# Two masked attention layers on one core: fewer, larger on-chip transfers, paired weighted sums, and a moved projection block

## The reference, cut to what matters

```
q = latents @ q_w + q_b ;  kv = [x, latents] @ kv_w + kv_b        # layer 0
attn = softmax(q k^T / 32, masked) ; o = attn @ v ; o @ out_w + out_b + residual
rmsnorm -> gelu MLP -> + residual
a = layer_norm(ctx) ; Q = h Wq^T ; K, V = a Wk^T, a Wv^T          # layer 1
softmax(Q K^T / sqrt(32), masked) @ V, then Wo^T, times tanh(gate), + h
```

## Time and profile before

| | |
|---|---|
| runs, median (lowest to highest) | 2631.36 us (2630.4 to 2631.77), 3 runs |
| profiled execution | 2632.31 us, its span 2630.5 us |
| busy in the span | PE 93%, PEld 73%, ACT 56%, DVE 44%, POOL 9% |
| layer 0, MLP, layer 1 | about 0 to 1070 us, to 1823 us, to the end |

### The profile page before, as it was taken

How to read it: one execution, slowest core, us unless ns; L and a number is a source line. 1 busy time by engine, 2 the same in 40 slices (tenths; PEclk the granted TensorE clock), 3 DMA queues, 4 the chain that set the end, 5 groups by cost and what they waited for, 6 DMA issues and landing times. The chain is left out here.

```text
span 2630.5 us, 43959 instructions
## 1 busy us (share of the span) xinstructions
PE 2443.7 (93%) x14528; PEld 1913.9 (73%) x14528; DVE 1170.5 (44%) x2222; ACT 1472.5 (56%) x3354; POOL 226.2 (9%) x252
## 2 busy tenths in 40 slices
PE   6999999999999999899999999998888888888887
PEld 5677777777777777478888888887767677676674
DVE  4455555555555555452212221122655455455553
ACT  3777777777777777552222222222556566566564
POOL 1000000000000000000000000001211112112110
PEclk8999999999999999799999999999999999999998
DMA  6555555555555555341101110121566665656655
GB/s 173 106 114 113 113 113 113 113 113 113 109 115 112 112 112 97 76 140 49 48 0 48 48 48 0 48 80 64 106 130 124 118 138 102 127 131 109 132 100 86
DMA packets 172764, 255.82 MB, mean 97 GB/s; under 512 B 33793, under 2 KB 84257, under 8 KB 172721
## 3 DMA queue, kind: packets, MB, share of 16 engines
q1 hardware_dynamic: 172720, 255.27, 45.3%
HBM read 86.28 MB, written 25.21 MB: 42 GB/s over the span
## 5 line engine op out<-in xcount | busy, mean ns | idle before, releaser
L531 ACT ACTIVATE l_score_ps<-l_score_ps,l_neg_max 128x512 f32<-128x512 f32 (+1 forms) x1024 | 566.6, 556 | 338.3 <-DVE l_neg_max L696 337.9
L696 DVE TENSOR_REDUCE l_neg_max<-l_score_ps 128x1 f32<-128x512 f32 (+1 forms) x768 | 494.6, 684 | 149.7 <-PE l_score_ps L934 149.3
L544 ACT ACTIVATE l_probs<-l_score_ps 128x1024 f32<-128x1024 f32 x384 | 385.0, 1020 | 104.5 <-PE l_score_ps L959 103.0
L934 PE MATMUL l_score_ps<-l_stack 97*128 97x512 f32 (+1 forms) x1024 | 326.9, 379 | 80.4 <-DMA l_stack<-mask_rows 53.2
L1220 ACT ACTIVATE mlp_hidden<-mlp_hidden_ps,mlp_b_col 128x512 f32<-128x512 f32 x128 | 88.3, 690 | 496.2 <-PE mlp_hidden_ps L66 496.0
L959 PEld LDWEIGHTS l_score_ps<-l_stack 99*128 99x128 f32 x1536 | 213.9, 194 | 156.5 <-issue 81.6
L1255 DVE TENSOR_TENSOR mlp_hidden_l<-mlp_hidden,mlp_hidden_h 128x512 fp32r<-128x512 f32 x128 | 93.7, 732 | 518.3 <-ACT mlp_hidden_h L1222 518.3
L959 PE MATMUL l_score_ps<-l_stack 99*128 99x256 f32 x1536 | 277.7, 308 | 40.7 <-ACT l_probs L544 25.4
L934 PEld LDWEIGHTS l_score_ps<-l_stack 97*128 97x128 f32 x1024 | 181.4, 202 | 126.3 <-ACT l_score_ps L531 63.3
L974 PE MATMUL l_o_ps<-l_probs,l_v 128*32 128x256 f32 x3072 | 244.5, 398 | 1.8
L713 DVE TENSOR_TENSOR l_o_norm<-l_o_ps,norm_room 128x256 f32<-128x256 f32 x128 | 54.4, 425 | 401.0 <-PE l_o_ps L974 318.1
(11 more groups left out here) (128 smaller groups left out, 4195.8 us busy)
## 6 DMA issues: line engine op xcount, KB each, us to landing
l_stack<-room SPq DMA_DIRECT2D x256, 192.0 KB
l_stack<-l_qk SPq DMA_DIRECT2D x256, 128.0 KB
l_stack<-room SPq DMA_DIRECT2D x128, 128.0 KB
norm_room<-l_shiftT SPq DMA_DIRECT2D x512, 32.0 KB, 4.0
l_stack<-l_qk SPq DMA_DIRECT2D x256, 64.0 KB
l_tokens<-in_x SPq DMA_DIRECT2D x16, 512.0 KB, 4.1
l_tokens<-in_ctx SPq DMA_DIRECT2D x16, 512.0 KB, 5.0
l_stack<-room SPq DMA_DIRECT2D x128, 64.0 KB
```

The costliest lines, as they stand in the source:

```text
L531: m = act.activation(e, e, ACT.Exp, bias=neg_max[:, q, h:h + 1], accum_out=row_sum[:, q, h:h + 1])
L544: act.activation(probs[:, s % PROBS, :].rearrange("p (a b) -> p a b", a=2), score_ps[:, 2 * (s % 2):2 * (s % 2) + 2, :], ACT.Exp).then_inc ...
L696: dve.tensor_reduce(out, bank, AXIS_X, ALU.max, negate=True).then_inc(max_done, 1)
L934: m = pe.matmul(out, stack[0:ROWS_MAX, h, P * q:P * (q + 1)], stack[0:ROWS_MAX, h, K_COLS], start=True, stop=True)
```

## The change

`load_stacks` becomes `load_group`: the columns of the query and key weights are stored permuted (`by_dim`), so that the four heads of a group lie on 128 partitions in the order of the stack, and one DMA moves what four DMAs moved for a half of the groups. A batch has 16 (layer 0) or 12 (layer 1) such DMAs in place of 32, and each group is loaded as soon as its own steps are done. The two shift DMAs of a half become one, the eight inverse DMAs two, each of four neighbouring rows spread over 128 partitions. The second pass goes by pairs of steps. In the last slot shifted 0 and 1 and `turn_shift` of half 1 stand ahead of the projection block, and ACT does exps 0, the copy, exps 1 ahead of the block's `high`. The permuted weights split in four DVE instructions instead of one, and layer 0's bias vectors load in 11 DMAs instead of 5.

```diff
-    PROBS = 3
+    PROBS = 4
-    STACK_DMAS = HG * 4 + 1
+    GROUP_DMAS = 4 if first else 3
+    STACK_DMAS = GROUP_DMAS * GROUPS + 1
...
+        def by_dim(w):
+            return w.rearrange("p f (g d j) -> p (f g) j d", d=DH, j=HG)
+        def by_head(w):
+            return w.rearrange("p f (g j d) -> p (f g) j d", d=DH, j=HG)
...
+                return [*[(bq[:, f:f + 1], q_b[f]) for f in range(FB)],
+                        *[(bk[:, f:f + 1], k_b[f, :, :, 0]) for f in range(FB)], (bv[:, :], kvb[:, :, 1]),
...
-        VECTORS = 5 if first else 3
+        VECTORS = 2 * FB + 3 if first else 3
-        INV_DMAS = HALF
+        INV_DMAS = GROUPS
...
-        def load_stacks(sp, b, half):
-            def move(slot, j, to_cols, src):
-                heads = slice(HALF * half + j, HALF * (half + 1), HG)
+        def load_group(sp, g):
+            half, heads = g // GROUPS, slice(HG * g, HG * (g + 1))
+            def move(slot, to_cols, src):
                 sp.dma_start(f32(stack[DH * slot:DH * (slot + 1), heads, to_cols]), f32(src)
                              ).then_inc(stack_loaded[half], 16)
+            if first:
+                move(0, Q_COLS, qk[:, g, Q_HIGH])
+                move(0, K_COLS, qk[:, g, K_HIGH])
+            else:
+                move(0, slice(0, WIDTH), qk[:, g, :].rearrange("p (n s) -> p n s", s=S)[:, 0:4:3, :])
+            move(1, slice(0, WIDTH), qk[:, g, 0:WIDTH])
+            move(2, slice(0, WIDTH), qk[:, g, WIDTH:2 * WIDTH])
...
-            def spread_inverse(a, half):
+            def spread_inverse(p, a, half):
+                if p is not None and half == HALVES - 1:
+                    sp.wait_ge(low_done, ITEMS * (p + 1))
...
-                for j in range(HALF):
-                    g, to = GROUPS * half + j // HG, slice(DH * (j % HG), DH * (j % HG + 1))
-                    sp.dma_start(inv_sum[to, g:g + 1, :],
-                                 shiftT[INV_ROW + j:INV_ROW + j + 1, half:half + 1, :].to_broadcast([1, DH, S])
+                for g in range(GROUPS * half, GROUPS * (half + 1)):
+                    row = INV_ROW + HG * (g % GROUPS)
+                    sp.dma_start(inv_sum[:, g, :], shiftT[row:row + HG, half:half + 1, :].to_broadcast([HG, DH, S])
                                  ).then_inc(inv_loaded[half], 16)
...
-                        for part in range(2):
-                            sp.dma_start(
-                                f32(stack[SHIFT_ROW + part:SHIFT_ROW + part + 1,
-                                          HALF * half:HALF * (half + 1), Q_COLS]),
-                                shiftT[HALF * part:HALF * (part + 1), half:half + 1, :],
-                            ).then_inc(shift_loaded[half], 16)
+                        sp.dma_start(f32(stack[SHIFT_ROW:SHIFT_ROW + 2, HALF * half:HALF * (half + 1), Q_COLS]),
+                                     shiftT[0:2 * HALF, half:half + 1, :]).then_inc(shift_loaded[half], 16)
...
-                            sp.wait_ge(shifted_done, PSTEPS * a + PSTEPS // HALVES * (half + 1))
-                        load_stacks(sp, p, half)
+                            sp.wait_ge(shifted_done, PSTEPS * a + KB * (g + 1))
+                        load_group(sp, g)
+                        if g % GROUPS == GROUPS - 1:
+                            load_mask(sp, p, g // GROUPS)
...
+                    if slot == SLOTS and a is not None:
+                        exps(a, 0)
+                        copy_shift(a, HALVES - 1)
+                        exps(a, 1)
...
+                    if slot == SLOTS - 1 and a is not None:
+                        shifted(a, 0)
+                        shifted(a, 1)
+                        turn_shift(a, HALVES - 1)
...
-                    for s in range(PSTEPS):
-                        if s + 2 < PSTEPS:
-                            shifted(a, s + 2)
+                    for s in range(0, PSTEPS, 2):
+                        for u in range(s + 2, min(s + 4, PSTEPS)):
+                            shifted(a, u)
                         weigh(a, s)
-                        if s >= KB and s % KB == KB - 1 and s < PSTEPS - 1:
-                            project(a, s // KB - 1)
+                        weigh(a, s + 1)
+                        if s >= KB and s % KB == KB - 2 and s < PSTEPS - 2:
+                            g = s // KB - 1
+                            if g == 0:
+                                if p is not None:
+                                    pe.wait_ge(low_done, ITEMS * (p + 1))
...
+                            project(a, g)
```

More of the change, by code:

```diff
@@ L236, in attention_layer @@
                     kv = stage[c].rearrange("p (f n two) -> p f n two", f=2, two=2)
[L237 to L240, removed]
+                    src, parts = kv[:, :, :, which], [t[:, 2 * c:2 * c + 2, :] for t in w]
+                    if w is wk:
+                        src, parts = by_head(src), [by_dim(t) for t in parts]
+                    split_ops.append((c, src, parts, 1.0))
+            staged = [stage[u % 2].rearrange("p (f n) -> p f n", f=FB) for u in range(4)]
+            split_ops.append((3, by_head(staged[3]), [by_dim(t[:, :, :]) for t in wq], SCALE))
+            split_ops.append((2, staged[2], [t[:, :, :] for t in wo], 1.0))
         else:
@@ L247, in attention_layer @@
                     n = FB * u + f
-                    split_ops.append((u, score_ps[:, n % RING, :], [t[:, f, :] for t in w], scale))
+                    src, parts = score_ps[:, n % RING:n % RING + 1, :], [t[:, f:f + 1, :] for t in w]
+                    if u < 2:
+                        src, parts = by_head(src), [by_dim(t) for t in parts]
+                    split_ops.append((u, src, parts, scale))
         last_op_of = [max(n for n, op in enumerate(split_ops) if op[0] == u) for u in range(len(raw))]
@@ L305, in load_tokens, with load_mask @@
             sp.dma_start(tokens[:, QT:2 * QT, :], c_view[b]).then_inc(tokens_loaded, 16)
-        def load_stacks(sp, b, half):
-            def move(slot, j, to_cols, src):
-                heads = slice(HALF * half + j, HALF * (half + 1), HG)
+        def load_group(sp, g):
+            half, heads = g // GROUPS, slice(HG * g, HG * (g + 1))
+            def move(slot, to_cols, src):
                 sp.dma_start(f32(stack[DH * slot:DH * (slot + 1), heads, to_cols]), f32(src)
                              ).then_inc(stack_loaded[half], 16)
[L313 to L318, removed]
+            if first:
[5 more added lines that the diff above has]
+            move(2, slice(0, WIDTH), qk[:, g, WIDTH:2 * WIDTH])
+        def load_mask(sp, b, half):
             sp.dma_start(f32(stack[MASK_ROW:MASK_ROW + 1, HALF * half:HALF * (half + 1), K_COLS]),
@@ L392, in iteration @@
                 if p is not None:
-                    for half in range(HALVES):
+                    for g in range(FB):
                         if a is None:
-                            sp.wait_ge(low_done, ITEMS * p + NT + NK + half + 1 if first
-                                       else ITEMS * p + NT + GROUPS * (half + 1))
-                        else:
-                            sp.wait_ge(shifted_done, PSTEPS * a + PSTEPS // HALVES * (half + 1))
-                        load_stacks(sp, p, half)
+                            sp.wait_ge(low_done, ITEMS * p + (NT + NK + g // 2 + 1 if first else NT + g + 1))
+                        else:
+                            sp.wait_ge(shifted_done, PSTEPS * a + KB * (g + 1))
+                        load_group(sp, g)
+                        if g % GROUPS == GROUPS - 1:
+                            load_mask(sp, p, g // GROUPS)
                 if a is not None and not first:
@@ L535, in copy_shift @@
                 act.wait_ge(shift_turned, HALVES * a + half + 1)
-                at_least(act, shift_loaded[half], 32 * a)
+                at_least(act, shift_loaded[half], 16 * a)
                 at_least(act, inv_loaded[half], 16 * INV_DMAS * a)
@@ L573, in iteration @@
                     if a is not None:
-                        for half in range(HALVES):
-                            if TURN_SLOT[half] == slot - 1:
-                                copy_shift(a, half)
+                        if TURN_SLOT[0] == slot - 1:
+                            copy_shift(a, 0)
                         if first and slot == AFTER_T:
@@ L588, in iteration @@
                 if a is not None:
-                    for s in range(PSTEPS):
+                    for s in range(2, PSTEPS):
                         exps(a, s)
@@ L625, in split_low @@
                 dve.wait_ge(w_high, n + 1)
+                if len(src.shape) == 4:
+                    for j in range(HG):
+                        m = dve.scalar_tensor_tensor(low[:, :, j, :], src[:, :, j, :], scale, f32(high[:, :, j, :]),
+                                                     ALU.mult, ALU.subtract)
+                    m.then_inc(w_low, 1)
+                    return
```

(19 more changed lines are left out.)

9 lines of the change are left out of this document (5 added, 4 removed).

## The result

The changed kernel takes 2827.53 us (2825.88 to 2828.26), the kernel before in the same comparison 2631.57 us: a ratio of 1.074, 95% interval 1.072 to 1.076. The forecast was 2677 (2560 to 2704): the right sign, a quarter of the size, and outside the range. The profiled execution of the changed kernel spans 2826.5 us.

What follows compares the result with a forecast made beforehand. TensorE's queue, busy 93% of the span, was taken to set the time. 2632.3 us profiled + 39 (layer 1) + 2 (layer 0) + 5 (setup) = 2678 profiled, 2677 as a median; range 2560 to 2704.

Steps and rivals of the forecast that it cites:

- Half a stack in layer 1 is 1.5 MB, 7.7 us at 201 GB/s: Layer 1's merged stack DMAs keep the old pace, so half 0 is in at 2250.9 and half 1 follows 7.7 us later.
- Stack half 0 is ready about when step 0 wants it: Layer 0's stack adds no wait at step 0; layer 0 in all +0.15 us a batch, +2 us for 15 batches.
- Pairs: Second pass, steps taken two at a time: 0.25 us less a pair, net -1.15 us a batch in layer 0, -0.75 in layer 1.
- The moved block: Projection block behind shifted 0 and 1: shifted 2 starts +0.6 us (0 to 1.2) in layer 0, 0 in layer 1.
- The merged inverses: Four-row spreads, two DMAs a half: 9.7 us a half at 27 GB/s, one DMA after the other.
- Shifted 4: Layer 1: TensorE waits 3.4 us for half 1's shift rows, queued behind half 0's inverses, in place of 1.01.
- step 0 of layer 1: Half 0 of the stack is in at 2250.9, so step 0 starts there, +3.2 us against 2247.7.
- Layer 1 in all: Layer 1 batch +2.6 us (+0.9 to +3.9), for 15 batches +39 us (14 to 58).
- The setup: Start of program: six more vector DMAs +4 us (0 to 9), weights split in four DVE pieces +1 (0 to 3).
- The first: Rival 1, faster: spreads still overlap, 7.2 us a half, 2583 us; read side by side 2541; chance 0.36.
- The second: Rival 2, slower still: new idle time keeps TensorE at 1.2 GHz for longer, +25 us, 2702 us; chance 0.09.

Runs made afterwards that it cites:

- the two-row set: Transfers alone, nothing of the reference computed: 256 KB of spreads as 4 DMAs of two rows each; measured at a DMA share of 0.12.
- the old set: Transfers alone, nothing of the reference computed: 2.36 MB in the old stack DMAs, 32 neighbouring partitions read and 32 written; 11.5 us.
- the slow sets: Transfers alone: 2.36 MB of 3 KB rows, reading every fourth or every second partition, or merged; 126 to 143 GB/s.

## Why the prediction was wrong

**The step that failed** is the one that gave the merged stack DMAs the old pace: "Half a stack in layer 1 is 1.5 MB, 7.7 us at 201 GB/s", and for layer 0 "Stack half 0 is ready about when step 0 wants it". The 201 GB/s were read off 16 DMAs that take 32 neighbouring partitions to 32; the new ones take 128 to 32. The trace of before did not show such an operation, and its price got no bounds, though the spreads beside it, of unseen shape too, did. Alone a half's 2.36 MB take 18.8 us instead of 11.5, and in the kernel 3 KB packets take 0.389 us against 0.229.

**Why that cost so much.** Counted from the issue of half 0's shift in layer 0, step 0 of the changed kernel wants its half at 34.1 us (590.08 - 6.21 - 549.77), of the kernel before at 33.0. The last landing of that half and the time when it is wanted, on the same count, over the nine to eleven batches of each trace between 290 and 1000 us:

| kernel | half 0 in | wanted | layer 0 batch |
|---|---|---|---|
| before | 28.9 to 29.1 | 33.0 | 66.0 |
| merged stack alone | 31.5 to 34.0 | 33.0 to 33.2 | 66.5 |
| pairs, block, merged inverses, old stack | 29.4 to 32.8 | 32.7 to 33.9 | 66.1 |
| every transfer cut up, new layout | 33.2 to 35.0 | 32.9 to 34.4 | 67.5 |
| the change with one-row spreads | 32.0 to 35.8 | 32.4 to 34.1 | 68.4 |
| the change with 16 stack DMAs | 34.7 to 37.2 | 32.9 to 34.1 | 71.3 |
| all of the change | 37.4 to 40.8, 40.3 in the batch above | 32.9 to 34.1 | 75.1 |

There were 4 to 5 us of slack. The slow stack uses up to 4.9 of them, the late inverses with pairs and block up to 3.7, and either alone is almost free in a layer 0 batch. Together they are 11.2 us, 6.2 past the need. That is 2.6 more than the two added. The packets account for it: the merged stack alone stood behind one-row spreads, at 0.32 us, and in the whole change it takes 0.389, and for 2.36 MB, 768 rows of 3 KB on 16 engines, that makes some 3 us (an estimate). Behind such a wait TensorE runs at 1.2 GHz in place of 2.4 for a while (a mean of 0.74 in this window):

```profile
590.00:597.00 7.00, 6.92 (x23) 5.58 (x24) 4.79 (x9) 4.47 (x13) 0.00 (x0) 0.74 1.05 130
```

In the changed kernel the inverses are in at 571.9, 22 us after the shift. At 201 GB/s a half would take 11.7 us from there (2.36 MB) and be in at 583.6, against a need of 583.9: with the old pace "about when step 0 wants it" would have been true, and in the run with the old stack in layer 0 alone the half is in 29.5 to 32.9 us after the shift. That run puts a size on it: 2827.5 - 2683.8 = 144 us, with 151 between forecast and result. In both layers the old stack takes back 178 us, and the 2649 us that are left are 28 under the forecast: the other terms together were too dear.

**By its other steps.** Pairs: layer 0 -1.2 a batch where -1.15 was forecast; layer 1 +0.1 where it was -0.75. There the stack set the end in any case, so that time won ahead of it became wait: the stack waits rose from 53.2 to 73.8 us. The moved block: +1.7 in layer 0 (66.5 against 64.8) where +0.6 stood, and +0.35 in layer 1 for 0; the mechanism, the wait for half 0's shift rows, was right, the wait 2.05 instead of 1.6, and the block gave nothing in return. The merged inverses: a set takes 9.6 us where 9.7 was taken, at 27 GB/s and a DMA share of 0.20. The Trainium skill, "DMA: Bandwidth & Descriptors", section "Why a DMA increments its semaphore by 16 and not by 1", said as much (4 engines of 16); the 0.21 in the window of the changed kernel and the two-row set, at a share of 0.12, agree with it too. Shifted 4 waits 2.52 us for 3.4, step 0 of layer 1 4.43. Layer 1 in all +3.6 a batch for the forecast's +2.6, and that nearness is partly luck. Counted from the issue of half 0's shift, half 1's inverses landed after 19.1 us (median of eleven batches) where the forecast had 22.0 (2242.7 - 2220.65; its sum for the stack starts from 2242.3, a slip of 0.4), and half 0 of the stack 12.5 behind them where it had 8.6 (7.7 + 0.9): two errors of opposite sign. With the old stack in both layers a batch takes 49.2 in place of 51.3, so 2.1 of the 3.6 are the slow stack, and the rest of the change costs 1.5, less than forecast. The setup: the vector DMAs issue in 7.1 us instead of 6.4, under 1 us; but the first step 0 starts at 63.6 instead of 55.0, 8.6 us for the 4 + 1 forecast. The cause is again the stack: with the merged stack alone it starts at 63.3, after a wait of 8.02.

**The rivals.** The first (spreads overlap, 2583) fell with the 9.6 us. The second had the right idea of a further loss at half clock, but as a part, not as the cause. None had the stack's own pace in it, and that is why the range missed.

## What to carry to other kernels

A DMA's pace belongs to its shape: the partitions that it reads, those that it writes, and how many rows its slowest dimension has. When a merge changes any of these, bound the pace anew, even if bytes and row length stay; a fill at full DMA share can be 1.6 times slower. Merging DMAs saves issue time on the queue. Here that paid in layer 1's stack (-1.4 us a batch, though the packets were slow) and not in layer 0's. Before calling a lateness free, write down the slack that hides it, and charge all the delays that draw on it together.

## What the runs showed of the hardware that was not expected

The same 2.36 MB between tiles, in rows of 3 KB, took 6.1 to 18.8 us by the choice of partitions, the merging included (128 partitions to the same 128, and 128 to 32). The Trainium skill, "SBUF — State Buffer", section "Door 1: The DMA port swizzle (why `[64,N]` ≈ `[32,N]`)", counts the ports that the partitions reach, some 27 GB/s each: 8 for 32 neighbours, 16 for every fourth or for all 128. It agrees with the old set (205 of 218 GB/s) and with 128 to 128 (386 of 435). Every fourth read and written stays under it too (304 of 435), with the engines busy for 0.76. It does not give the slow sets: by the ports of their narrower side they too should reach 218, and they moved 126 to 143. That engines meet different neighbours at the two ends fits these numbers, but which engine moved which row isn't in the trace, so this cause is argued, not shown.

Two sets on one queue hardly overlap, though one of them uses few engines: spreads of four rows, at a share of 0.20, and the old set behind them took 22.0 us together, 9.6 and 11.5 alone.
